# The 64-row last chunk of the FFN packed into whole 128-wide tiles

## What is computed

```
x = x + tanh(g_xattn) * xattn(layernorm(x), ctx)      # 32 heads of 8, queries and keys RMS-normalised
x = x + tanh(g_ffn)   * ffn(layernorm(x))
gate = silu(h @ Wgate.T); up = h @ Wup.T              # 256 -> 704
ffn  = (gate * up) @ Wdown.T                          # 704 -> 256
```

## Time and profile before

| | |
|---|---|
| median of 3 runs | 267.28 us (266.71 to 267.42) |
| profiled execution | 267.05 us, of it the span 265.2 us |
| mean granted TensorE clock | 0.942 |
| PE busy | 219.6 us (83%), 2592 matmuls |
| DVE busy | 176.5 us (67%) |
| ACT busy | 177.8 us (67%) |
| POOL busy | 106.3 us (40%) |
| matmuls of the chunks (L1363), 64 wide | 64, of 384 |
| matmuls of `down` over 64 rows (L1388, L1407) | 32, of 192 |

### The profile page before, as it was taken

The page is one execution under the profiler, slowest core; times in us unless marked ns, Lnnn a source line. Parts: engine busy times, 40 slices in busy tenths (PEclk is TensorE's granted clock), DMA queues, the critical chain, the costliest instruction groups (busy, mean ns, idle before and its releaser), DMA issues.

```text
span 265.2 us, 7329 instructions
## 1 busy us (share of the span) xinstructions
PE 219.6 (83%) x2592; PEld 178.5 (67%) x2592; DVE 176.5 (67%) x583; ACT 177.8 (67%) x338; POOL 106.3 (40%) x145
## 2 busy tenths in 40 slices
PE   1663979659879999899989989998999697965864
PEld 1553758437657878688777868786878585855764
DVE  4487999934665776687658765876596674657162
ACT  3258585844867895789578867885897667534250
POOL 5012212021322463645464455446444735434451
PEclk9999597956988999999999999999999999996799
DMA  5897522233075022603160406050506070000001
GB/s 178 216 352 178 62 56 49 54 45 62 0 101 101 0 56 49 136 3 72 26 138 0 87 12 138 0 100 3 121 0 82 13 109 2 21 22 0 20 20 40
DMA packets 45127, 18.08 MB, mean 68 GB/s; under 512 B 36400, under 2 KB 44848, under 8 KB 45104
## 3 DMA queue, kind: packets, MB, share of 16 engines
q1 hardware_dynamic: 45104, 17.77, 31.6%
HBM read 7.28 MB, written 2.10 MB: 35 GB/s over the span
## 4 chain that ended last, share of the span: by engine, by line
DVE 30%; PE 29%; issue 15%; POOL 14%; ACT 7%; DMA 2%; SPq 1%; DVEq 1%; POOLq 0%; ACTq 0%
PE bank L1278 7%; PE bank L1363 5%; POOL qk_parts L422 4%; POOL qk_unit L462 4%; PE pv_ps L1242 4%; POOL h_lo L430 4%; PE bank L1388 3%; DVE sums L899 3%; DVE hidden L990 3%; PE score_ps L1223 2%; PE bank L1311 2%; DVE silu L975 2%; DMA w_raw<-L_xattn_Wv_dram 2%; POOL x_all L439 2%; PE bank L1265 2%
## 5 line engine op out<-in xcount | busy, mean ns | idle before, releaser
L526 ACT ACTIVATE probs<-score_ps 128x1024 f32<-128x1024 f32 x64 | 65.9, 1032 | 3.5 <-PE score_ps L1223 3.5
L1363 PE MATMUL bank<-x_hi,gu_hi 128*128 128x256 f32 (+1 forms) x192 | 51.0, 301 | 4.7 <-DVE hidden L990 2.0
L462 POOL TENSOR_TENSOR qk_unit<-qk_raw,root_y 128x512 f32<-128x512 f32 x16 | 17.4, 1085 | 85.4 <-DVE root_y L783 85.4
L1363 PE MATMUL bank<-x_lo,gu_hi 128*128 128x256 f32 (+1 forms) x192 | 48.4, 286 | 0.0
L1242 PE MATMUL pv_ps<-probs,v_blocks 128*32 128x128 f32 x1024 | 42.8, 286 | 6.2 <-issue 4.2
L430 POOL TENSOR_TENSOR h_lo<-hidden,h_hi 128x256 fp32r<-128x256 f32 (+1 forms) x48 | 35.3, 745 | 24.8 <-ACT h_hi L651 24.4
L1363 PEld LDWEIGHTS bank<-x_hi,gu_hi 128*128 128x128 f32 (+1 forms) x192 | 35.3, 184 | 9.5 <-DVE hidden L990 2.4
L1363 PEld LDWEIGHTS bank<-x_lo,gu_hi 128*128 128x128 f32 (+1 forms) x192 | 35.5, 185 | 0.0
L1242 PEld LDWEIGHTS pv_ps<-probs,v_blocks 128*32 128x32 f32 x1024 | 24.9, 112 | 15.5 <-issue 7.4
L640 ACT ACTIVATE tanh_g<-bank,half_gate 128x256 f32<-128x256 f32 (+1 forms) x48 | 22.8, 475 | 18.2 <-PE bank L1363 16.0
L1278 PE MATMUL bank<-w_hi,xc_hi 128*128 128x256 f32 x96 | 31.7, 330 | 2.4 <-DVE xc_lo L889 2.4
(11 more groups left out here) (108 smaller groups left out, 435.2 us busy)
## 6 DMA issues: line engine op xcount, KB each, us to landing
ctx_sb<-ctx_dram SPq DMA_DIRECT2D x16, 128.0 KB, 2.6
out_dram<-x_all SPq DMA_DIRECT2D x16, 128.0 KB, 1.8
x_all<-x_dram SPq DMA_DIRECT2D x1, 1536.0 KB, 10.5
dn_int<-L_ffn_wq_down_dram SPq DMA_DIRECT2D x1, 704.0 KB, 6.7
gu_int<-L_ffn_wq_gate_dram SPq DMA_DIRECT2D x1, 640.0 KB, 4.6
gu_int<-L_ffn_wq_up_dram SPq DMA_DIRECT2D x1, 640.0 KB, 5.7
x_all<-x_dram SPq DMA_DIRECT2D x1, 384.0 KB, 5.1
w_raw<-L_xattn_Wq_dram SPq DMA_DIRECT2D x1, 256.0 KB, 2.7
```

Of the source, the lines that this page charges most:

```text
L462: nc.gpsimd.tensor_tensor(qk_unit[:], qk_raw[:], root_y[:, 0:2 * H].unsqueeze(2).to_broadcast([P, 2 * H, HD]), ALU.mult).then_inc(unit_rea ...
L526: nc.scalar.activation(probs[:, t % 2, :], score_ps[t % 2][:].rearrange("p h n -> p (h n)"), ACT.Exp, scale=float(HD) ** 0.5 / UNIT ** 2). ...
L1363: last = nc.tensor.matmul(bank[k][0:r, a * TOK:(a + 1) * TOK], w[:, j, a, c, 0:r], xx[:, c, :], start=(n == 1), stop=(n == (4 if wide_weig ...
```

## The change

Only the last chunk (j = 5, `LAST` = 64 rows) changes.

- Its weights for gate and up lie side by side in one 128-wide tile of `gu_hi` (`gate_up_columns`), so `chunk` makes both with 4 matmuls in place of 8. Gate lands in PSUM partitions 0 to 63, up in 64 to 127, both in columns 0 to 255.
- `silu2`, the third scale, `hidden` and `h_hi` of this chunk lie in partitions 64 to 127 (`hidden_rows`). DVE's `gate` reads partitions 0 to 63 and writes 64 to 127.
- POOL writes the lower piece of the chunk not to `h_lo` but to partitions 0 to 63 of `h_hi`, so that one 128-row tile holds both pieces. `dn_hi` holds the 64 weight rows of this chunk twice (`down_rows`). `down` takes 1 matmul over 128 rows in place of 2 over 64.
- POOL waits for its own previous subtraction ahead of this one, and for this one behind it.
- In the preparation of the weights, ACT and DVE each make one more 64-row copy.

```diff
+        def hidden_rows(j):
+            return slice(0, P) if j < NJ - 1 else slice(LAST, 2 * LAST)
+        def gate_up_columns(w, j):
+            if j < NJ - 1:
+                return w[:, j, :, :, :]
+            return w[:, j, 0, :, :].rearrange("p c (a n) -> p a c n", a=2)
+        def down_rows(j):
+            return (0,) if j < NJ - 1 else (0, LAST)
```

POOL, in `split_hidden`:

```diff
-                nc.gpsimd.tensor_tensor(h_lo[0:r, j, :], hidden[0:r, j % 3, :], h_hi[0:r, j, :].bitcast(F32),
+                of = hidden_rows(j)
+                lower = h_lo[:, j, :] if j < NJ - 1 else h_hi[0:LAST, j, :]
+                if j == NJ - 1:
+                    pool.wait_ge(h_lo_ready, n)
+                nc.gpsimd.tensor_tensor(lower, hidden[of, j % 3, :], h_hi[of, j, :].bitcast(F32),
                                         ALU.subtract).then_inc(h_lo_ready, 1)
+                if j == NJ - 1:
+                    pool.wait_ge(h_lo_ready, n + 1)
```

ACT, in `upper` and in its `prep` (DVE's `prep` changes in the same way):

```diff
-                nc.scalar.copy(h_hi[0:r, j, :], hidden[0:r, j % 3, :]).then_inc(h_hi_ready, 1)
+                of = hidden_rows(j)
+                nc.scalar.copy(h_hi[of, j, :], hidden[of, j % 3, :]).then_inc(h_hi_ready, 1)
...
-                    last = nc.scalar.copy(dn_hi[0:rows(j), j, :], bank[k][0:rows(j), a * D:(a + 1) * D])
+                    for at in down_rows(j):
+                        last = nc.scalar.copy(dn_hi[at:at + rows(j), j, :], bank[k][0:rows(j), a * D:(a + 1) * D])
```

DVE, in `gate` and `up`:

```diff
-                nc.vector.scalar_tensor_tensor(out=silu2[0:r, j % 2, :], in0=tanh_g[0:r, j % 2, :], scalar=1.0,
+                nc.vector.scalar_tensor_tensor(out=silu2[hidden_rows(j), j % 2, :], in0=tanh_g[0:r, j % 2, :], scalar=1.0,
...
-                nc.vector.scalar_tensor_tensor(out=hidden[0:r, j % 3, :], in0=silu2[0:r, j % 2, :], scalar=scales[0:r, 2, j:j + 1],
-                                               in1=bank[k][0:r, TOK:2 * TOK], op0=ALU.mult, op1=ALU.mult).then_inc(drained[k], 1)
+                of = hidden_rows(j)
+                half = slice(TOK, 2 * TOK) if j < NJ - 1 else slice(0, TOK)
+                nc.vector.scalar_tensor_tensor(out=hidden[of, j % 3, :], in0=silu2[of, j % 2, :], scalar=scales[of, 2, j:j + 1],
+                                               in1=bank[k][of, half], op0=ALU.mult, op1=ALU.mult).then_inc(drained[k], 1)
```

PE, in `chunk`, and the products of `down` and `down_last`:

```diff
-                for a in range(2):
+                for a in range(2 if j < NJ - 1 else 1):
...
-                            last = nc.tensor.matmul(bank[k][0:r, a * TOK:(a + 1) * TOK], w[:, j, a, c, 0:r], xx[:, c, :],
+                            last = nc.tensor.matmul(bank[k][:, a * TOK:(a + 1) * TOK], w[:, j, a, c, :], xx[:, c, :],
...
+            def down_products(wide_weights, j):
+                if j < NJ - 1:
+                    return products(wide_weights, dn_hi, dn_lo, h_hi, h_lo)
+                return [(dn_hi, h_hi), (dn_lo, h_hi)] if wide_weights else [(dn_hi, h_hi)]
```

More of the change, by code:

```diff
@@ L1005, in prep @@
                     j = 2 * (part - NJ) + a
[L1006 to L1007 removed]
+                    for at in down_rows(j):
+                        last = nc.vector.tensor_tensor(dn_lo[at:at + rows(j), j, :], bank[k][0:rows(j), a * D:(a + 1) * D],
+                                                       dn_hi[0:rows(j), j, :].bitcast(F32), ALU.subtract)
                 last.then_inc(drained[k], 1)
```

29 lines of the change are left out of this document (10 added, 19 removed).

## The result

The changed kernel takes 279.28 us (median; 274.87 to 280.34) where the kernel before, run beside it, takes 267.35 (266.71 to 271.48). The ratio is 1.038, with a 95% interval of 1.025 to 1.051: slower, as forecast, but by 12 us between the medians (10 by the ratio), where I had 2.6 and a range that ended at 273.2.

A forecast was written before the change was run, and what follows sets the result against it. A cycle through PE, ACT, POOL and DVE was taken to bound the loop, 1.15 us longer than PE's work. 267.05 + 0.6 chain + 4.3 clock - 2.1 end = 269.85, forecast as 269.9 us; range 264.9 to 273.2.

The forecast's parts named there:

- PE's saving lies off the cycle: Loop: chunk 5 and `down` save PE 1.23 us an iteration, hidden by the cycle except what chunk 5 gives ACT.
- what the forecast named as signs in the changed profile: Loop: pause over 2 us, clock stretches at 0.50 near the transposes, POOL self-wait, iterations 25.9 to 26.1 us without a fall.
- POOL's waits, +0.25 an iteration: Loop, between POOL's subtractions and `x_all`: two new waits on its own results add 0.25 to 0.30 us, taken as 0.25.
- My upper bound of 0.5: Loop, POOL's two new self-waits: at most 0.38 plus a few register steps, 0.5 us an iteration.
- ACT's gain of 0.12: Loop: tanh of chunk 5 can start earlier on ACT, gaining 0.06 to 0.18 us an iteration, taken as 0.12.
- DVE's held instructions: DVE around chunk 5: overlap of 0.08 lost up to three times a pair, 0.24 us, hidden in the loop; 0.1 in p = 7.
- The net term: Loop: POOL's added waits net of ACT's gain, +0.13 us an iteration.
- the 0.6 of the sum: Chain total: +0.13 us four times in the loop and about 0.1 in p = 6, +0.6 us.
- The clock in the loop: PE's longer pause makes the clock fall at 3 of 5 boundaries from p = 2 to p = 7, 1.5 us each: +4.3 us.
- the third fall: End of p = 6, the longest pause, expected 3.2 us or more: one clock fall, priced at 1.5 us.
- The end of the kernel, -2.1: Tail, PE on the path: p = 7 -0.7, p = 8 -1.0, `down_last` -0.4, together -2.1 us.
- POOL costs more: Rival: the subtraction across partitions takes half again its 0.76, +0.4 us in each of five iterations, 271.9 us; chance 0.07.

The follow-up runs named there:

- run 14: Kernel before plus only POOL's two waits around the 64-row subtraction, with 12 idle matmuls in PE's pause: 267.59 us, ratio 1.000.
- run 13: Kernel before with fewer PE products in chunk 5 and the last chunk of `down`, plus 14 idle matmuls in PE's pause: 271.37 us, ratio 1.014.
- run 12: Changed kernel with `x_all` moved ahead of chunk 5's subtraction and its waits, plus 12 idle matmuls in PE's pause: 268.74 us, ratio 1.000.
- run 3: Changed kernel with 12 idle matmuls added in PE's pause: 269.91 us, ratio 1.015.
- run 6: Changed kernel with a shorter chain: DVE finishes `attn` ahead of `qk_double`, POOL adds it right behind chunk 3: 269.05 us, ratio 1.001.
- run 4: Kernel before with only POOL's two waits around its 64-row subtraction: 272.43 us, ratio 1.021.
- the second profile: Changed kernel measured again, unaltered: 277.08 us, ratio 1.035; the profiled execution took 276.0 us.
- run 8: Changed kernel with `attn` ahead of `qk_double` and its addition right behind chunk 3, plus 12 idle matmuls in PE's pause: 263.81 us, ratio 0.987.
- run 7: Kernel before, unpacked, with `attn` taken ahead of `qk_double` and its addition right behind chunk 3: 263.53 us, ratio 0.986.
- run 10: Run 9 with 20, 10 and 12 idle matmuls in three pauses of the last two pairs: 262.25 us, ratio 0.975.
- run 5: Changed kernel with POOL's `x_all` moved ahead of chunk 5's subtraction, so neither new wait stands ahead of it: 275.41 us, ratio 1.022.
- run 9: Run 8 with ACT squaring the second tile's queries and keys ahead of normalizing the next tile: 262.04 us, ratio 0.978.
- run 2: Changed kernel with PE work put back: chunk 5 multiplied twice, 3 or 4 unused matmuls behind each `down`: 269.78 us, ratio 1.014.
- run 11: Kernel before with 8 idle matmuls in PE's pause: 267.49 us, ratio 1.000.
- run 1: Kernel before with only less PE work: products left out in chunk 5 and the last chunk of `down`: 270.17 us, ratio 1.013.

## Why the prediction was right in direction and wrong in size

- **PE's saving lies off the cycle: right.** PE works 22.9 us in 25.7 and no period of the changed kernel became shorter than 25.8. Most of what the forecast named as signs in the changed profile came: falls as PE starts again, and a self-wait on POOL. The pause itself did not reach the 2 us that it named (1.70 to 1.92), and periods without a fall took 26.3, not 25.9 to 26.1.
- **POOL's waits, +0.25 an iteration: short by a third.** Alone they cost 0.39 (run 14): 0.27 behind the subtraction, 0.09 ahead of it, and the overlap of some 0.04 that back-to-back operations have. My upper bound of 0.5 held them; my choice didn't.
- **ACT's gain of 0.12: wrong in sign.** `h_hi` did come 0.17 earlier (run 13: 0.18), and brought POOL's subtraction onto DVE's copy. Alone that lengthens the period by 0.2 (run 13).
- **DVE's held instructions, "the loop hides it": half right.** The price of 0.24 for them was what they cost; the copy's 0.35 on top was in no term. POOL's waits cover nearly all of it (5.11 against 5.06), but without them it would show (run 12). The net term was +0.13 an iteration; measured with the clock up it is 0.4. Over the whole stretch to the end of p = 6 that is 2.0 us (1.7 in the four periods, 0.2 behind them, rounded), for the 0.6 of the sum.
- **The clock in the loop: mechanism right, its sum right by luck.** Idle work in the pause takes away the falls of each kernel that it was put into, and with them 2.3% (6 us) of the changed kernel's time by the ratios (run 3), 1.4% of run 6's and 2.1% of run 4's. A fall of 3.4 us cost 1.0 to 1.5 us (priced at 1.5), but one of the two in the changed kernel's loop lasted 6.8 us and cost 2.6, which I had not counted on although such stretches stood in the trace of before. The loop lost 4.2 us to two falls, where 4.3 was forecast for three. The two numbers agree by luck: the third fall was to come at the longest pause, 2.48 us at the end of p = 6, and the clock held there (in the second profile it fell for 6.8 us). So the length of a pause doesn't tell by itself whether a fall comes, and what else does stays open.
- **The end of the kernel, -2.1: the step that failed.** It came out at +0.9. I took the shorter `down` as won time and applied the clock's reaction to pauses up to p = 7's start alone. The stretch begins at the transposes behind the end of p = 6 (211.84 before), and its first part ends at the next such ones, before:

```profile
233.34 0.55 PE L1311 MATMUL bank<-ident,o_turned 128*128 128x128 f32 x3 [0.96 <-DVE hidden L990]
```

and with the change:

```profile
218.74 0.55 PE L1335 MATMUL bank<-ident,o_turned 128*128 128x128 f32 x3 [2.48 <-DVE hidden L1013]
...
241.07 0.55 PE L1335 MATMUL bank<-ident,o_turned 128*128 128x128 f32 x3 [0.96 <-DVE hidden L1013]
```

| part | forecast | measured | falls, before | falls, changed |
|---|---|---|---|---|
| p = 7 | -0.7 | +0.8 | none | 3.4 at 231.3 |
| p = 8 and 9, up to `down_last` | -1.0 | -1.1 | 6.8 | 6.8 |
| `down_last` | -0.4 | +1.2 | none | 3.4 at 265.4 |

What PE saves was sized right: in run 8, without a fall there, p = 7 takes 20.9 us against the 21.5 of its unpacked counterpart, run 7, and in run 10 `down_last` goes from its first to its last product in 2.6 us, against 3.0 in the kernel before and 4.1 in the changed one. What the term left out are two falls of some 1.5 us each, behind pauses that PE's shorter work had made longer (1.34 to 1.61 and 1.51 to 2.03 us). For the second the profiles speak with one voice: ahead of `down_last` the clock fell in all eight that have a pause of 2.0 us there (the changed kernel twice, runs 3, 5, 6, 8, 9, 12) and held in all six with 1.5 us (the kernel before, runs 2, 4, 7, 11, 14). For the first they don't: run 8 has the pause of 1.61 us too, and no fall.

- **Ahead of the loop: +0.8**, not in the sum. PE idled once inside a score group, without anything that the profile could name:

```profile
58.38 0.39 PE L1247 MATMUL score_ps<-q_stack,k_stack 32*128 32x128 f16 x3 [1.42 <-issue]
```

In the profile's own terms, 274.87 for 269.85, the miss of 5.0 us is 3.0 from the end, 1.4 from the chain (2.0 for 0.6, rounded) and 0.8 from ahead, less 0.2 from the falls of the loop. (The 0.23 us between profile and median, named behind the sum, was not added to it; with it the forecast would have been 270.1.) The median's further 4.4 us over the profiled execution is not explained: run 5, which has a fall at all four boundaries and 111.2 in the loop, shows that the loop can take 2 us more, but no profile of the changed kernel caught such an execution. The two longest ones, 279.83 and 280.34, had a mean granted clock of 0.882 and 0.889 for the profiled one's 0.924, so more of their time was at the low clock; where it lay isn't on record.

Of the rivals, "POOL costs more" was nearest in kind, though not for its reason: the subtraction across partitions takes 0.72, not more than the plain one.

## What to carry to other kernels

When work taken from an engine is not on the path, ask what its longer pause does before calling it free: here TensorE's clock fell around its longer pause, and 1.4 us of idle matmuls in it were worth 4 to 6 us by the ratios (5 to 9 by the medians). Shorten the chain that makes the engine wait first (taking `attn` ahead of three copies and its addition ahead of two subtractions gave 0.7 us a period without packing and 1.1 with it, and then the packed and the unpacked kernel are equal), and judge the tail by the same rule as the loop. Where executions scatter, cut the traces at fixed places and compare the pieces: the loop repeated to 0.4 us in kernels whose medians couldn't be told apart.

## What the runs showed of the hardware

- Falls of the granted clock came in stretches of 3.4 and 6.8 us in the loop, ahead of it also of 10.2 and 13.7. With a fall of 3.4 us at each boundary, 27.3 us apart, the periods of run 1 took 27.2 to 27.4, the last 26.8, for a chain of 26.05; those of run 5, with falls as far apart, took 27.5 to 27.7, and 28.4 with the fall of 6.8.
- Pauses of 1.10 to 1.22 us never brought it down in the loop of before, 1.3 us did at two boundaries of four (run 6), 1.5 to 1.6 us at one of four (run 4), 1.7 to 1.9 us at two of four (changed kernel), 1.8 to 2.0 us at each in run 1. At the end of p = 6 it fell at a pause of 1.17 us in run 12 and held at one of 2.48 us in the changed kernel. Ahead of `down_last` it fell with 2.0 us in eight profiles of eight and held with 1.5 us in six of six, but in run 1 it held there with 1.90. So the length alone doesn't decide; what else does was not tested.
- A DVE copy of 128x256 within SBUF took 0.27 to 0.28 us when POOL was idle at its start (run 8; also before, 0.16 us ahead of a subtraction), 0.62 when it began 0.28 us behind the start of a POOL subtraction (changed kernel), and 0.86 when it began 0.02 us behind it (run 13): each of the last two ended 0.15 us behind the subtraction. Of the two copies of 128x128 behind it the first took 0.21 to 0.22 us in all of them, the second 0.76 beside a subtraction and 0.22 without one. That the two engines share something was not tested by itself.
- DVE instructions whose partitions start elsewhere than those before them began without overlap: 0.24 us more for the three around chunk 5 (1.48 for 1.24).
- A wait of POOL for its own last result cost 0.27 us here, not the 0.19 of the row that I had taken it from.
